# Nystrom attention's pseudo-inverse loop: where the two halves of the output products of the sample before stand in TensorE's queue

## The reference

```python
def _pinv(a, iters=6):
    z = swapaxes(a) / (col * row)
    for _ in range(iters):
        az = a @ z
        z = 0.25 * z @ (13 * I - az @ (15 * I - az @ (7 * I - az)))
    return z
...
attn1, attn2, attn3 = softmax(q @ k_l.T), softmax(q_l @ k_l.T), softmax(q_l @ k.T)
a12 = attn1 @ _pinv(attn2)
out = a12 @ (attn3 @ v)
out = out + depthwise_conv(v, res_kernel)      # 33 taps along the tokens
out = out.transpose(...) @ w_out + b_out
```

## Time and profile before

| | us |
|---|---|
| median of 3 runs | 703.7 |
| the runs | 701.5, 703.7, 717.6 |
| span of the profiled execution, first to last instruction | 699.5 |
| busy in that span: TensorE matmul | 657.6 (94%) |
| VectorE | 407.5 (58%) |
| ScalarE | 374.8 (54%) |
| GpSimd | 229.5 (33%) |
| mean granted clock of TensorE | 0.979 |

### The profile page before, as it was taken

The page is one execution under the profiler, slowest core; times in us unless marked ns, Lnnn a source line. Parts: engine busy times, 40 slices in busy tenths (PEclk is TensorE's granted clock), DMA queues, the critical chain, the costliest instruction groups (busy, mean ns, idle before and its releaser), DMA issues. The chain is left out here.

```text
span 699.5 us, 15186 instructions
## 1 busy us (share of the span) xinstructions
PE 657.6 (94%) x6053; PEld 505.3 (72%) x6053; DVE 407.5 (58%) x832; ACT 374.8 (54%) x1033; POOL 229.5 (33%) x204
## 2 busy tenths in 40 slices
PE   9988999999999999999989999689999999999895
PEld 5777788898989898989855555466666666657555
DVE  3557475857585857675742333347777777764331
ACT  4666684747465555565255555235555455546431
POOL 4074444445353535444300451033232222201001
PEclk9999999999999999999999999959999999998999
DMA  8200000000000000000000000000000000000000
GB/s 272 113 2 3 1 1 2 3 1 2 1 2 2 1 2 2 1 2 2 1 1 1 1 1 1 0 1 2 1 1 1 1 0 2 1 0 1 1 17 17
DMA packets 5214, 8.23 MB, mean 12 GB/s; under 512 B 3608, under 2 KB 4120, under 8 KB 4760
## 3 DMA queue, kind: packets, MB, share of 16 engines
q1 hardware_dynamic: 4552, 7.20, 3.2%
q10 hardware_dynamic: 592, 0.07, 0.1%
HBM read 6.71 MB, written 0.55 MB: 10 GB/s over the span
## 5 line engine op out<-in xcount | busy, mean ns | idle before, releaser
L1333 POOL TENSOR_TENSOR STD<-STD,NN 91x492 f32<-91x492 f32 (+1 forms) x96 | 104.2, 1100 | 147.2 <-DVE NN L1486 80.7
L1486 DVE SCALAR_TENSOR_TENSOR NN<-ST,PS 91x492 f32<-91x492 f32 x96 | 62.7, 659 | 54.5 <-PE PS L940 54.2
L940 PE MATMUL PS<-ST 128*91 128x123 f32 x768 | 92.6, 271 | 1.9 <-DVE ST L1495 1.8
L940 PE MATMUL PS<-NN 128*91 128x123 f32 (+1 forms) x768 | 89.8, 267 | 2.1 <-DVE NN L1486 2.1
L940 PEld LDWEIGHTS PS<-ST 128*91 128x91 f32 x768 | 83.5, 159 | 7.3 <-DVE ST L1495 2.7
L940 PEld LDWEIGHTS PS<-NN 128*91 128x91 f32 x768 | 81.1, 159 | 10.2 <-DVE NN L1486 6.6
L1980 PE MATMUL PS<-QR,KA 128*128 128x270 f32 x256 | 71.8, 411 | 0.0
L1495 DVE SCALAR_TENSOR_TENSOR ST<-PS,STD 91x492 f32<-91x492 f32 (+1 forms) x96 | 56.4, 599 | 26.4 <-POOL STD L1333 18.5
L2096 DVE TENSOR_SCALAR CL<-PS,K 128x270 f32<-128x270 f32 x144 | 65.7, 496 | 9.5 <-PE PS L1980 4.1
L1212 ACT ACTIVATE STD<-ST 91x492 f32<-91x492 f32 (+1 forms) x96 | 51.1, 571 | 33.5 <-DVE ST L1495 33.4
L2037 ACT ACTIVATE EX<-CL,NG 128x540 f32<-128x540 f32 x64 | 46.8, 743 | 32.7 <-DVE CL L2096 32.6
(11 more groups left out here) (347 smaller groups left out, 1211.4 us busy)
## 6 DMA issues: line engine op xcount, KB each, us to landing
TP<-taps SPq DMA_DIRECT2D x1, 1204.0 KB, 15.7
MA<-mat SPq DMA_DIRECT2D x1, 1120.0 KB, 7.4
MF<-mat SPq DMA_DIRECT2D x1, 1024.0 KB, 12.7
WI<-wide SPq DMA_DIRECT2D x1, 902.0 KB, 8.9
CO<-const SPq DMA_DIRECT2D x1, 512.0 KB, 15.1
MQ<-mat SPq DMA_DIRECT2D x1, 512.0 KB, 15.9
out<-OS SPq DMA_DIRECT2D x8, 45.0 KB
XA<-xpatch SPq DMA_DIRECT2D x1, 256.0 KB, 3.1
```

Source lines behind the costliest of these rows:

```text
L940: last = nc.tensor.matmul(PS[0:NL, PINV + q, h % 4 * SW + c0:(h % 4 + 1) * SW], x[:, h, 0:NL], x[:, h, c0:SW], start=True, stop=True)
L1333: nc.gpsimd.tensor_tensor(TD[:, 4 * q:4 * q + 4, c0:SW], SA[:, 4 * q:4 * q + 4, c0:SW], NN[0:NL, 4 * q:4 * q + 4, c0:SW], ALU.subtract).th ...
L1486: v.scalar_tensor_tensor(out=NN[0:NL, own, :], in0=ST[0:NL, b % 2, own, :], scalar=N_S, in1=heads4(PS[0:NL, PINV + q, 0:4 * SW]), op0=ALU. ...
```

## The change

In TensorE's loop, attend(b-1, 1) is called behind step 3, right behind attend(b-1, 0), and no longer behind step 4. Behind step 4 nothing is left for samples 1 to 7. No instruction and no semaphore is added or removed, and the queues of the other engines are unchanged.

```diff
                 FIRST = {1: lambda b: (project(b), values(b)), 3: scores3, 6: scores1, 8: lambda b: turn3(b, 0), 9: lambda b: turn3(b, 1),
                          10: weigh, 11: turn_weighed}
-                BACK = {3: lambda b: attend(b, 0), 4: lambda b: attend(b, 1), 6: out_proj}
+                BACK = {3: lambda b: (attend(b, 0), attend(b, 1)), 6: out_proj}
```

## The result

The changed kernel's median is 709.4 us in 6 runs (707.7 to 716.3), that of the kernel before 704.9 in 6 runs (701.2 to 717.6). The ratio leaves out two slow runs of the kernel before (713.9 and 717.6), so its base is the median of the other four, 702.6 us: it is 1.010, with an interval of 1.0071 to 1.0129, that is 7.0 us slower (5.0 to 9.1).

A forecast was written before the change was run, and what follows sets the result against it. TensorE's queue was taken as the bound, only just, at 33.49 of 33.85 us a sample. Six samples at 1.00 us each added 6.0 us to 703.7, giving 709.7 us, range 704.5 to 713.5.

The forecast's parts named there:

- the price of a sample: Delay added to each of samples 1 to 6: 1.00 us, with bounds of 0.81 and 1.12 us.
- the forecast's base of 703.7: Median time of the kernel before, in us, to which the forecast added 6.0 us.
- Behind step 3: TensorE's queue: added cover buys nothing, and step 4 starts one half of attend later, 1.00 us (at most 1.12).
- behind step 4: TensorE's queue: step 5 loses its cover but itself waits at most 0.1 us; the delay comes out further on.
- What is late next: Everything fed by step 4, through VectorE and GpSimd to step 9, moves by 1.00 us less what is covered.
- The walk: Sample 3 followed link by link from step 4's NN through TD, L1400, ST and top1 to step 9: 1.00 us.
- top1 and NN of step 6 are 1.00 us late as well: VectorE after ST of step 5: both pass on the full 1.00 us, so step 7 starts at 200.24.
- the second idle: TensorE's wait before step 7, released by NN: about 0.45 us.
- VectorE first: Rival: L1400 issues before the second TD, which is held instead; 0.43 to 0.79 us a sample, 706.3 to 708.4; chance 0.13.
- TensorE's queue alone: Rival: VectorE's delay is absorbed before step 6, only saved breaks on TensorE show, 1.4 us, giving 702.3 us; chance 0.08.
- Slower by over 2%: Rival: 14 us, 2.35 us in each of six samples, through a lower granted clock; chance 0.04.
- A larger loss on ScalarE: Rival: missed waits on ScalarE between steps 6 and 9, 1.2 to 2.3 us a sample, 711 to 717.5; chance 0.07.

The follow-up runs named there:

- Filling the empty place: Changed kernel with scores1 moved from behind step 5 to behind step 4: 34.68 us a sample, against 34.70 for the changed kernel.
- the other order: Kernel before with both halves of attend behind step 4 and none behind step 3: 33.97 us a sample, against 33.85.
- the kernel before without the hold: Kernel before with total3's two two-operand instructions (L1400, L1403) replaced by one-operand reciprocals: 33.84 us a sample, against 33.85.
- The changed kernel without the hold: Changed kernel with total3's two two-operand instructions (L1400, L1403) replaced by one-operand reciprocals: 34.09 us a sample, against 34.70.
- moving such an instruction behind the work that someone waits for: VectorE's total1 and inverse1 moved behind the second half of step 8's NN: 33.28 us a sample from the kernel before, 34.12 from the changed one.

## Why the prediction was right, and where its steps were off

**The time.** 709.7 us was forecast and 709.4 measured, within the range; the ratio gives 7.0 us (5.0 to 9.1), the forecast 6.0. Of this the profiles show 6 x 0.85 = 5.1 us in samples 1 to 6 and 0.17 us back in sample 7, 4.9 us in all. That is at the interval's lower end; the rest goes with the granted clock behind the loop. Runs at the same mean clock show it. At 0.977 the changed kernel's two runs have spans of 705.8 us, and eight runs of the kernel before (of the 17 above) have 701.7 to 702.1, so 3.7 to 4.1 us less; at 0.974 it is 706.8 and 707.7 against 702.5, 4.3 and 5.2 us. A thousandth of the mean clock goes with about 1.2 us (an estimate from spans of about 699.3 at 0.979 and 701.9 at 0.977), so by the last digit of the clock these differences agree with the loop's 4.9. Five of those 17 runs stand at 0.979, and none of the changed kernel's eight; whether the change makes the clock fall more often behind the loop, or that is chance, stays open. So the closeness of 709.7 is in part luck: the price of a sample was put 0.15 us too high, and runs at a lower clock made up for it in the median. The changed kernel's two runs at 0.977 took 707.7 us, 4.0 above the forecast's base of 703.7.

**Behind step 3 and behind step 4.** As forecast: step 4 comes 0.98 us later (1.00 forecast), step 5 follows it with no wait, and the delay comes out further on. Filling the empty place gave nothing back. The pair saves 0.14 us of breaks (1.00 us for its first half); of the 0.08 us that a rival put between steps 4 and 5 only 0.02 are there (1.84 us against 1.86 with filler). In the other order bare step 3 made TensorE wait 0.17 us. So that a bare step costs nothing was seen for even steps (0 and 4) and not for the odd one.

**What is late next.** The walk held link by link: TD released by NN and 0.81 us late, as forecast ((195.44 - 181.21) - (193.20 - 179.78)); L1400 held to TD's end and L1403 at 0.16 us; ST of step 5 late by (198.00 - 181.21) - (195.58 - 179.78) = 0.99 us (1.00 forecast); 0.64 us idle before step 6 (0.7 forecast). The step that failed is the next, "top1 and NN of step 6 are 1.00 us late as well". top1 starts 17.95 us into the sample instead of 17.09, 0.86 us later. Before, it waited for scores1 and not for ST. The row of scores1 in TensorE's timeline of the kernel before:

```profile
195.94 0.86 PE L843 MATMUL PS<-KM,QM 32*71 32x91 f32 x32
```

It ended at 196.80, and top1 started at 196.87. That it was scores1 shows in the kernel before without the hold, where ST's second half ends 0.07 us earlier, at 196.74, and top1 starts as late as ever (VectorE's timeline):

```profile
196.07 0.67 DVE L1493 SCALAR_TENSOR_TENSOR ST<-PS,STD 91x492 f32<-91x492 f32 x1 [0.18 <-PE PS L940]
196.89 1.74 DVE L1392 TENSOR_REDUCE M<-PS 71x8 f32<-71x728 f32 x2 [0.15 <-PE PS L843]
```

Behind ST alone top1 could have started about 0.14 us earlier: in the changed kernel, where nothing else holds it, it starts 0.08 us ahead of ST's recorded end (199.16 against 199.24), and before 0.06 us behind it. So some 0.13 us of the delay are taken up there, the second idle is 0.26 us instead of 0.45, step 7 comes 20.30 us into the sample instead of 19.45, and a sample loses 0.85 us and not 1.00. ST ended 0.01 us from scores1, and the prediction took the wrong one for the releaser.

**The rivals.** *VectorE first* didn't happen: L1400 lost in all six samples. The changed kernel without the hold shows that rival's path, ST's second half waiting for TD alone, at 0.24 us a sample and not the 0.43 to 0.79 that it was priced at; ST ends 0.40 us later there, and again some of that is taken up at top1. *TensorE's queue alone* is refuted by the waits before steps 6 and 7. *Slower by over 2%:* the mean clock of all three changed profiles is lower than before (0.962, 0.974 and 0.970 against 0.979), but it fell behind the loop; in the loop it is 1.00. A larger loss on ScalarE didn't come.

**The rule on SBUF's shared port** (the Trainium skill, page "SBUF — State Buffer", section "Who interferes with whom") agrees here: instructions with two SBUF operands stand to TD's end, 1.10 us instead of 0.16, while reciprocals with one operand pass at 0.20 us.

## What to carry to other kernels

The price of filler moved on a queue isn't the gap it leaves, but how late the next link starts on the engine with the least slack; so follow the moved step's result to the next join of two inputs and ask which came last, and by how much. Where two inputs end within 0.1 us of each other, either can be the releaser, and a delay can cost less than the chain says. A small instruction on VectorE beside a long one on GpSimd can be the link that passes a delay on, and moving such an instruction behind the work that someone waits for won 0.57 us a sample here, while neither of the two other orders of attend won anything.

## What was not expected of the hardware

- A shown wait of 0.35 us of TensorE, in the middle of a step, was worth 0.57 us when it was taken away.
- A VectorE instruction with a single SBUF tensor (L1424, 71 x 16) is stretched beside GpSimd's TD just as those with two are, to 1.12 us in the changed kernel and 0.98 us where it came later (0.11 us in sample 0, where no TD runs beside it), while a reciprocal of the same size isn't: L1423 takes 0.25 us.
